# One Trainium2 core: log-posterior sums and expert-input normalising on GpSimd, a plain f32 first expert product, and scatters spaced by a new rule

## The reference, cut to what matters

```python
# 1: token layer: the gradient of a soft Needleman-Wunsch alignment score (a posterior, 32 x 128 x 128)
h = jax.vmap(jax.grad(nw_value, argnums=0))(theta, A)
# 2: attention over each of the 8 x 512 rows, 8 heads of 16, scores -(q - k)^2
h = h + attention(layernorm(h), Wq, Wk, Wv, Wm)
# 3: mixture of experts on x = layernorm(h): 8 experts, each token goes to the best 2
topv, topi = top_k(x @ Wg, 2)
w = softmax(topv)                         # two gate weights per token
for e in range(8):
    y += gw[..., e:e+1] * ((silu(x @ W[e]) * (x @ V[e])) @ W2[e])   # W, V: 128 x 512; W2: 512 x 128
h = h + y
```

## Time and profile before

| | |
|---|---|
| median of 3 runs | 653.98 us (653.51 to 655.54) |
| the profiled execution | 656.17 us |
| its span in the trace | 654.4 us |
| mean granted TensorE clock | 0.941 |
| busy share of PE, DVE, ACT, POOL | 58%, 68%, 61%, 51% |
| DMA traffic | 54.20 MB, mean 83 GB/s |

### The profile page before, as it was taken

How to read it: one execution, slowest core, us unless ns; L and a number is a source line. 1 busy time by engine, 2 the same in 40 slices (tenths; PEclk the granted TensorE clock), 3 DMA queues, 4 the chain that set the end, 5 groups by cost and what they waited for, 6 DMA issues and landing times. The chain is left out here.

```text
span 654.4 us, 13131 instructions
## 1 busy us (share of the span) xinstructions
PE 381.7 (58%) x3169; PEld 310.4 (47%) x3169; DVE 444.1 (68%) x1539; ACT 397.9 (61%) x1176; POOL 334.4 (51%) x510
## 2 busy tenths in 40 slices
PE   4200000000015677767798877899988599999990
PEld 2200000000002555655566656787877478888880
DVE  4499999999958688999977844666554123333651
ACT  3266656665715887797889924666454246556660
POOL 1097979797934355563365540343545633443331
PEclk9999999999999987887988778999999979999996
DMA  5269954233654233344000110121222211125524
GB/s 111 52 138 176 158 110 89 41 65 64 144 128 129 80 114 113 113 123 109 18 30 23 38 47 13 38 50 42 59 56 74 76 41 47 54 65 156 153 62 112
DMA packets 113287, 54.20 MB, mean 83 GB/s; under 512 B 57102, under 2 KB 108942, under 8 KB 113061
## 3 DMA queue, kind: packets, MB, share of 16 engines
q1 hardware_dynamic: 103758, 43.49, 29.1%
q0 software_dynamic: 4320, 8.47, 3.9%
q10 hardware_dynamic: 5136, 1.41, 1.0%
HBM read 29.61 MB, written 24.19 MB: 82 GB/s over the span
## 5 line engine op out<-in xcount | busy, mean ns | idle before, releaser
L1780 DVE TENSOR_TENSOR sq<-sq,ps 128x512 f32<-128x512 f32 x71 | 48.8, 688 | 118.8 <-ACT sq L1156 66.1
L1338 POOL DMA_INDIRECT y_dram<-ybuf,dest x71 | 69.6, 980 | 84.0 <-ACT ybuf L1170 68.8
L1295 POOL DMA_INDIRECT xd_dram<-pay,slot x64 | 61.8, 966 | 89.4 <-ACT sq L1156 53.8
L1255 POOL TENSOR_TENSOR D<-D 128x256 f32<-128x256 f32 x130 | 95.3, 734 | 0.0
L752 PE MATMUL ps<-zdiag,ones_f 32*128 32x32 f32 x2 | 0.6, 406 | 161.1 <-DVE zdiag L1496 161.1
L899 PE MATMUL ps<-wdn,xnt 128*128 x568 | 77.6, 281 | 8.7 <-ACT ybuf L1170 8.6
L1118 ACT ACTIVATE sq<-sq,mn 128x128 f32<-128x128 f32 x256 | 78.0, 392 | 0.0
L752 PEld LDWEIGHTS ps<-zdiag,ones_f 32*128 32x128 f32 x2 | 0.5, 305 | 161.4 <-DVE zdiag L1496 161.4
L899 PEld LDWEIGHTS ps<-wdn,xnt 128*128 128x128 f32 x568 | 70.6, 196 | 10.6 <-issue 10.5
L1247 POOL TENSOR_TENSOR D<-D 128x64 f32<-128x64 f32 x130 | 39.9, 307 | 47.1 <-DVE D L1440 46.4
L1024 ACT ACTIVATE D<-D 64x2 f32<-64x2 f32 (+1 forms) x154 | 31.1, 202 | 53.6 <-DVE D L1440 42.4
(11 more groups left out here) (239 smaller groups left out, 1111.2 us busy)
## 6 DMA issues: line engine op xcount, KB each, us to landing
stage<-xd_dram SPq DMA_DIRECT2D x71, 65.0 KB
D<-th_dram SPq DMA_DIRECT2D x14, 208.0 KB, 5.0
g_dram<-D SPq DMA_DIRECT2D x14, 208.0 KB, 4.6
x_dram<-D SPq DMA_DIRECT2D x14, 208.0 KB, 4.7
stage<-in_w_up SPq DMA_DIRECT2D x8, 256.0 KB, 3.3
stage<-in_v_up SPq DMA_DIRECT2D x8, 256.0 KB, 2.9
wdn<-in_w_down SPq DMA_DIRECT2D x8, 256.0 KB, 5.1
out<-thf SPq DMA_DIRECT2D x8, 256.0 KB
```

The source lines that it names most:

```text
L1255: pool.tensor_tensor(C3[:, k, :, :].rearrange("p (r d) c -> p r d c", d=2), bass.AP(tensor=m.tensor, offset=m.offset, ap=[m.ap[0], [H + 1, ...
L1295: pool.indirect_dma_start(xd_dram, bass.IndirectOffsetOnAxis(slot[:, q, j, k:k + 1], 0), pay[q % 3][:, k, j, :], None).then_inc(s_sc[2 * k ...
L1338: pool.indirect_dma_start(y_dram, bass.IndirectOffsetOnAxis(dest[:, w:w + 1], 0), yrow[w], None, bounds_check=2 * NB * T - 1, oob_is_err=F ...
L1780: V_.tensor_tensor(hid[c % 2], act_up[c % 2], ps[:, 4, :], ALU.mult).then_inc(s_hid, 1)
```

## The change

Five edits. On POOL, `log_posterior(q)` for q = 1 to 7 and `normed_inputs(q)`, which writes both payload copies at step `norms`; `weights` and `copy_inputs` are gone. DVE keeps the last steps of 1/sqrt. SP loads the 16 weight matrices straight to `wspace`, in f32. In the experts, ACT copies the gate half and DVE the other half of the tile's weights to `wtile`, at an address taken from a register; PE makes 8 plain f32 products of 128x128 with a block of weights stationary and the token columns moving, so that the hidden tile comes out transposed already; `turn`, `hidden_turned` and `column_low` are gone; in step k PE does up(k), column(k+1), down(k-1). Scatters wait for another count. Read backs of rows start 3 tiles later and follow more closely.

```diff
-        HALF_READ = HALF_DONE + 7
-        MORE_READ = MORE_DONE + 9
+        HALF_READ = HALF_DONE + 10
+        MORE_READ = MORE_DONE + 12
-                   **{MORE_READ + 2 * (q - HALF // 4): q for q in range(HALF // 4, MORE // 4)}}
-        ADD_AT = {k + 4: q for k, q in READ_AT.items()}
-        STORE_AT = {MORE_READ + 2 * q: q for q in range(HALF // 4)}
+                   **{MORE_READ + q - HALF // 4: q for q in range(HALF // 4, MORE // 4)}}
+        ADD_AT = {k + 2: q for k, q in READ_AT.items()}
+        STORE_AT = {HALF_READ + 7 + 2 * q: q for q in range(HALF // 4 - 1)}
...
             def load_weights(c):
-                need(sp, s_whi, c - 1)
-                need(sp, s_wlo, c - 1)
-                sp.dma_start(stage[c % 2][:], (w_up, v_up)[kind][e]).then_inc(s_stage[c % 2], 16)
+                need(sp, s_sq, c - 3)
+                sp.dma_start((wup, vup)[kind][:, e, :], (w_up, v_up)[kind][e]).then_inc(s_wu, 16)
...
-            def up(k, c, e):
+            def up(k, c):
                 pe.wait_ge(s_xc, k + 1)
-                pe.wait_ge(s_xcl, k + 1)
-                for n, hi, lo, free in ((3, wup_hi, wup_lo, s_silu), (4, vup_hi, vup_lo, s_hid)):
-                    m = three(ps[:, n, :], (xcol_hi[c % 2], xcol_lo[c % 2]),
-                              [w[:, bass.ds(e, 1), :].rearrange("p e f -> p (e f)") for w in (hi, lo)])
+                for half, (free, copied_to) in enumerate(((s_silu, s_wg), (s_hid, s_wv))):
+                    w = wtile[c % 2][:, half, :]
+                    pe.wait_ge(copied_to, k + 1)
+                    for n in range(FC):
+                        m = nc.tensor.matmul(ps[:, 3 + half, T * n:T * n + T], w[:, T * n:T * n + T], xcol[c % 2],
+                                             start=True, stop=True)
...
-            def turn(k, c):
-                for n in range(FC):
-                    m = nc.tensor.transpose(ps[:, 5, T * n:T * n + T], hid[c % 2][:, T * n:T * n + T], eye_sb[:])
...
-            def hidden_turned(k, c):
-                nc.scalar.activation(hidt[c % 2][:], ps[:, 5, :], ACT.Copy).then_inc(s_ht, 1)
+            def gate_weights_of(k):
+                e = act.value_load(tili[0:1, 1, k:k + 1], min_val=0, max_val=NX - 1)
+                need(act, s_up, 2 * k - 3)
+                nc.scalar.activation(wtile[k % 2][:, 0, :], wup[:, bass.ds(e, 1), :].rearrange("p e f -> p (e f)"),
+                                     ACT.Copy).then_inc(s_wg, 1)
...
-            def copy_inputs(q):
-                pool.wait_ge(s_x3, q + 1)
-                pool.tensor_copy(pay[q % 3][:, :, 1, 0:E], pay[q % 3][:, :, 0, 0:E]).then_inc(s_x3c, 1)
+            def log_posterior(q):
+                if q == 0:
+                    return
+                h = h0q[q % 2]
+                pool.wait_ge(s_e2, q)
+                pool.wait_ge(s_ldq[q % 2], 32 * (q // 2 + 2 - q % 2))
+                for k in range(4):
+                    m = pool.tensor_scalar(h[:, k, :], h[:, k, :], nvt[:, 4 * q + k:4 * q + k + 1], None, ALU.add)
+                m.then_inc(s_shifted, 1)
+                pool.wait_ge(s_shifted, q)
+                pool.tensor_tensor(h[:], h[:], gb[q % 2][:, :, ::-1], ALU.add).then_inc(s_e2, 1)
+            def normed_inputs(q):
+                pool.wait_ge(s_nrm, q + 1)
+                pool.wait_ge(s_h1, q + 1)
+                need(pool, s_sent, q - 2)
+                for j, done in ((0, s_x3), (1, s_x3c)):
+                    for k in range(4):
+                        m = pool.tensor_scalar(pay[q % 3][:, k, j, 0:E], h1[:, 4 * q + k, :], mv[:, 1, k, 0:1], r1[:, 1, 0, k:k + 1],
+                                               ALU.subtract, ALU.mult)
+                    m.then_inc(done, 1)
+            def rows_before_scatter(k):
+                return k + 14 if k < 18 else max(k + 1, 32 + 2 * (k - 18) // 3)
             def scatter(k, w):
-                pool.wait_ge(s_y, max(k + 1, BEHIND + 3 * k // 4))
+                pool.wait_ge(s_y, rows_before_scatter(k))
...
                     if n == SENT_AT[q]:
                         sent(q)
-                back(copy_inputs, n, 'turned')
+                front(log_posterior, n, 'logs')
+                back(normed_inputs, n, 'norms')
                 front(inputs_normed, n, 'norms')
                 send(n, 0)
-                if 0 <= n + 1 < CHUNKS:
-                    weights(n + 1)
...
+            def up_weights_of(k):
+                e = dve.value_load(tili[0:1, 1, k:k + 1], min_val=0, max_val=NX - 1)
+                need(dve, s_up, 2 * k - 2)
+                V_.tensor_copy(wtile[k % 2][:, 1, :], vup[:, bass.ds(e, 1), :].rearrange("p e f -> p (e f)")).then_inc(s_wv, 1)
             def dve_tile(k, c, w, tail=0):
+                if tail < 1:
+                    up_weights_of(k + 1)
                 if tail < 2:
                     hidden(k, c)
-                if tail < 1:
-                    column_low(k + 1, (c + 1) % 4)
```

More of the change, by code:

```diff
@@ L156, in tower @@
         align.close()
-        wup_hi, wup_lo, vup_hi, vup_lo = (
-            sb(n, [128, NX, F], fr) for n in ("wup_hi", "wup_lo", "vup_hi", "vup_lo"))
+        wspace = sb("wspace", [128, 4 * NX, F])
+        wup, vup = wspace[:, 0:NX, :], wspace[:, NX:2 * NX, :]
+        wtile = [wspace[:, 2 * NX + 2 * k:2 * NX + 2 * k + 2, :] for k in range(2)]
         wdn = sb("wdn", [128, NX, FC, E])
-        def parts_of(c):
-            kind, e = c // NX, c % NX
-            staged = stage[c % 2][:]
-            hi, lo = ((wup_hi, wup_lo), (vup_hi, vup_lo))[kind]
-            return hi[:, e, :], lo[:, e, :], staged
         h0q1 = sb("h0q1", [T, 4, T])
@@ L232, in tower @@
         yrow = [ybuf[:, k, :] for k in range(YR)]
-        xcol_hi = [sb(f"xcol_hi{k}", [128, T], fr)[:, :] for k in range(2)]
-        xcol_lo = [sb(f"xcol_lo{k}", [128, T], fr)[:, :] for k in range(2)]
+        xcol = [sb(f"xcol{k}", [128, T])[:, :] for k in range(2)]
         act_up = [sq[0][:, F * k:F * k + F] for k in range(2)]
         hid = [sq[1][:, F * k:F * k + F] for k in range(2)]
-        hidt = xnt
         dest = sb("dest", [128, YR], i32)
@@ L281, in tower @@
         s_qkh = sem("s_qkh")
-        s_stage = [sem(f"s_stage{k}") for k in range(2)]
-        s_whi = sem("s_whi")
-        s_wlo = sem("s_wlo")
+        s_wu = sem("s_wu")
+        s_wg = sem("s_wg")
+        s_wv = sem("s_wv")
         s_wd = sem("s_wd")
@@ L288, in tower @@
         s_rkc = sem("s_rkc")
-        s_xcl = sem("s_xcl")
         s_const = sem("s_const")
@@ L324, in tower @@
         s_x3c = sem("s_x3c")
+        s_nrm = sem("s_nrm")
+        s_shifted = sem("s_shifted")
         s_x3tp = sem("s_x3tp")
@@ L696, in _ @@
                     store_out(STORE_AT[k])
-            for q in range(HALF // 4, MORE // 4):
+            for q in range(HALF // 4 - 1, MORE // 4):
                 store_out(q)
@@ L706, in _ @@
         def _(pe):
-            def three(dst, a, b, first=True, last=True):
-                nc.tensor.matmul(dst, a[0], b[0], start=first, stop=False)
-                nc.tensor.matmul(dst, a[0], b[1], start=False, stop=False)
-                return nc.tensor.matmul(dst, a[1], b[0], start=False, stop=last)
             pe.wait_ge(s_in, 16 * 6)
@@ L918, in expert_of @@
                 return pe.value_load(tili[0:1, 1, at_tile(k)], min_val=0, max_val=NX - 1)
-            def pe_tiles(first, count):
-                places = range(count)
-                expert = {0: expert_of(first)}
-                for n in places:
-                    k, c = first + n, n % 4
-                    if not isinstance(k, int) or k < TILES:
-                        up(k, c, expert[n])
-                    if not isinstance(k, int) or k + 1 < TILES:
-                        column(k + 1, (c + 1) % 4)
-                    if n < 2 and (not isinstance(k, int) or k >= 2):
-                        expert[n - 2] = expert_of(k - 2)
-                    if not isinstance(k, int) or 1 <= k < TILES + 1:
-                        turn(k - 1, (c + 3) % 4)
-                    if n + 1 < count and (not isinstance(k, int) or k + 1 < TILES):
-                        expert[n + 1] = expert_of(k + 1)
-                    if not isinstance(k, int) or k >= 2:
-                        down(k - 2, (c + 2) % 4, expert[n - 2])
             pe.wait_ge(s_const, 16 * 10)
@@ L960, in _ @@
                     column(0, 0)
+                    expert[0] = expert_of(0)
                 if k >= 1:
-                    turn(k - 1, (k + 3) % 4)
-                if k >= 2:
-                    down(k - 2, (k + 2) % 4, expert.pop(k - 2))
+                    down(k - 1, (k + 3) % 4, expert.pop(k - 1))
                 back(ranks, n, 'ranks')
-            pe_tiles(UNROLLED, TILES - UNROLLED + 2)
+            for k in range(UNROLLED, TILES + 1):
+                if k < TILES:
+                    up(k, k % 4)
+                if k + 1 < TILES:
+                    column(k + 1, (k + 1) % 4)
+                    expert[k + 1] = expert_of(k + 1)
```

(12 more changed lines are left out.)

72 lines of the change are left out of this document (24 added, 48 removed).

## The result

The changed kernel took 672.02 us (median of 4 runs, 666.07 to 674.94) against 654.16 us for the kernel before: a ratio of 1.0259, 95% interval 1.0186 to 1.0331. The interval lies wholly above 1. The forecast was 644 us, range 631 to 658. Its profiled execution took 671.45 us, with a span of 669.5 us.

A forecast was written before the change was run, and what follows sets the result against it. No single engine bounds the attention (DVE, later ACT); PE alone limits the last expert stretch. Terms -6 + 2.5 + 0 + 0 - 4.8 - 2.1 = -10.4 give 645.8, less 2.2 for the median: 644 us, range 631 to 658.

The forecast's parts named there:

- Norms on POOL in the midst of the sends: End of attention: quad 5's eight normalising instructions among quad 3's sends cost 4.0 us, net +2.5; later norms nothing.
- credit of 1.5: End of attention: splitting eight sends into four and four pauses ACT and PE less, giving back 1.5 us.
- Log posterior to POOL: Attention: relieving DVE gains 13 us, a later exponential on ACT costs 7; net -6, bounds -13 and +3.
- The weight parts that POOL no longer makes: Attention: dropping this work only helps POOL, which isn't the limit in either stretch; gain nothing.
- Tile before the bursts, 0 to 34: Expert tiles 0 to 34: copies swapped on ACT, DVE's added copy hides; sum 0, bounds -2 and +7 us.
- theory E: Experiments' rival explanation: the new expert products with their weight copies slow tiles 0 to 34; expert part alone 660 to 670 us.
- Steady tile: Expert tiles behind the burst: PE needs 2.78 us, a loop through ACT 2.86; no change, bounds -2 and +14.
- Rival A: Experts: ACT's loop sets the tile's period, 2.98 us or more, making the kernel slower, up to 658; chance 0.16.
- Scatters: Experts: spacing scatters removes a burst (-11.4 us) but groups of three cost 6.6 more; net -4.8, bounds -11.4 and 0.
- rival B: Experts: the spaced scatters don't pause anything, so 6.6 us more go: 637 us; chance 0.22.
- Tail: From the last tile's first product to its rows: 6.7 us becomes 4.6, so -2.1, bounds -1 and -3.
- Rival D: Experts: DVE's new weight copy in each tile delays POOL's sends and scatters, +6 us: 650; chance 0.08.

## Why the prediction was wrong, step by step

- **"Norms on POOL in the midst of the sends": +2.5, bounds 0 and +4, then "nothing, bounds 0 and +3". This is the step that failed.** It cost 24.9 us (chip B; 3.3%, 20.4 us, on chip A). Four things in it were wrong. The duration: 0.81 us and not 0.50, taken from a row with the same name, shape and engine but with multiply then add where the new line has subtract then multiply; that alone is 16.5 us. The quads: only 5, 6 and 7 were priced. The norms of quads 0 to 4 stand in POOL's stream during the attention, and there they went in at nothing, without a reason; the changed kernel is 8.9 us behind at the attention's end on chip B. The sends: they waited behind the true 6.2 us and the 2.4 us wait for DVE's roots, and PE was idle 10.96 us before tile 0. The credit of 1.5 did have its ground, since ACT's longest idle time with a "remote" releaser at that place fell from 7.36 to 2.07 us, but it was outweighed. And what I did not price: PE's transposes of these rows, one step behind in PE's stream, wait for POOL (8.3 us in the changed kernel's trace at L820, 0.4 with the norms on DVE); two of these waits, 2.12 and 2.84 us, stand between tiles, the others ahead of tile 0. How much of the loss is theirs is not shown.
- **"Log posterior to POOL": -6, bounds -13 and +3.** Measured +6.0 (chip B, norms on DVE), beyond the upper bound. The gain of 13 was built on DVE's busy time as if a fuller engine were always the one waited for; that this is why it did not come is argued, not shown. What I priced as a delay of ACT's exponential was there (it starts right behind POOL's last addition), but 3.5 us of the 6.0 is one quad's work ahead of the first keys, a place I had not looked at.
- **"The weight parts that POOL no longer makes ... nothing."** Wrong, and to the good: the expert part alone gives 1.0% on chip B, and 5.2 us ahead of tile 0 in its trace. DVE's four-part sum gets faster by a quarter (602 to 450 ns) with them gone, so the 16.9 us (28 instructions) that I meant to win by moving it was 12.6 by then. That the earlier trace rows show DVE held up beside POOL should have led there. No run takes away the weight parts alone, so how much of the 5.2 us is this sum is not shown.
- **"Tile before the bursts, 0 to 34": 0, bounds -2 and +7.** With the norms on DVE: 516.8 - 392.3 = 124.5 against 119.9, +4.6 on chip A, inside; the expert part alone has +4.3 on chip B. So the sum of 0 was a few us too low, and theory E had a part; which of the copies or waits makes it was not looked for. Of the changed kernel's +18.3 the other 13.7 are the failed step, again.
- **"Steady tile": 2.78 against a loop of 2.15 + x with x = 0.71.** Right for PE's work; the forecast took the loop's 2.86 and no change, and the period is 2.79 where it was 2.84. In the timeline below silu starts at 634.59 and the weight copy at 635.25, so x is 0.66 and the loop by that sum 2.81. But PE has no idle time before its product at 636.29, and ACT waits 0.53 us for PE ahead of silu: PE's work of 2.78 sets the period, and the loop fits beside it. Rival A's wait is seen twice between 606 and 649 us (3.0 us of PE's idle time for ACT's column), not in each tile.

```profile
633.50 1.95 PE L861 MATMUL ps<-xcol,wspace 128*128 128x128 f32 x16
...
634.59 0.60 ACT L1111 ACTIVATE sq<-ps 128x512 f32<-128x512 f32 x1 [0.53 <-PE ps L861]
...
635.25 0.63 ACT L1128 ACTIVATE wspace<-wspace 128x512 f32 x1
...
635.78 0.26 ACT L1105 ACTIVATE xcol<-ps 128x128 f32<-128x128 f32 x1
...
636.29 1.95 PE L861 MATMUL ps<-xcol,wspace 128*128 128x128 f32 x16
```

- **"Scatters": -4.8, bounds -11.4 and 0.** The old rule costs 1.5% on chip A, so the term is near its lower bound: rival B, with a chance of 0.22, was right on this point, the groups of three cost little. It holds for chips that pause; on chip B it is zero.
- **"Tail": -2.1.** 669.5 - 650.4 = 19.1 against 654.4 - 633.4 = 21.0: -1.9, right.
- **Rival D**, DVE's weight copy holding up POOL's DMAs: the expert part alone, which has these copies, loses nothing in sum. Its scatters land 2.3 us after issue, as in the kernel before (median, both on chip B), its sends 2.5 us after it (2.4), and each keeps POOL for 0.98 to 1.00 us (0.97 to 0.98). So nothing in the runs supports it; the few us in tiles 0 to 34 are open, as said.
- **The range.** The bounds of the failed step came from one row and left the form of the instruction out; no rival had the norms as its mechanism. What came out right beside it (the scatters, the tail, the tile's period) could not make up for it.

With both vector parts back on DVE the change is 1.1% faster than the kernel before on chip B (not run so on chip A, where the norms alone back gave 0.7%). Of the kernels run here that is the one to keep on chip B; the expert part alone, at 1.0%, is as good within the intervals.

## What to carry to other kernels

Moving work off a busy engine is priced at the queue that takes it: list what stands behind the moved instructions there, and what stands behind their result on a third engine's in-order stream, and price each at the place, not by busy shares. A row gives the duration of its own form only; before it is lent to a new line, compare the operations inside it as well as shape and type. And when work on one engine goes away, look for the other engine that it was slowing.
